# A hybrid block on one core: buffers shared across phases, residual rows added to beta by their transfer, last group stored by tiles

## The chip, the cores and the metric

The kernel runs on one core of one Trainium2 chip. The metric is the device time of one execution in microseconds (us). Five engines run their own instruction streams: TensorE (PE, with its weight loads as PEld), VectorE (DVE), ScalarE (ACT), GpSimd (POOL) and SyncE (SP). They meet only through semaphores. Transfers are issued by SP, ACT or POOL and carried out by 16 DMA engines that all queues share.

## The reference, cut to what matters

```python
x = attn_a(x)      # Mamba-2 style mixer: 16 heads of 64, state 64
x = ffn(x)         # below
x = attn_b(x)      # mixer: 64 heads of 16, state 128
x = ffn(x)         # the same weights again

# ffn, per batch b of 4, 1024 rows of 512, fp32
x1     = layer_norm(x)                                   # rows of x
t      = layer_norm(last row of x1, in_gamma, in_beta)
th     = t @ agg_w + agg_b
for step in range(4):                                    # K_STEPS
    n  = layer_norm(th, pn_gamma, pn_beta)
    th = th + gelu(n @ d1_w + d1_b) @ d2_w + d2_b        # d1_w 512x2048, d2_w 2048x512
msg    = th @ bc_w + bc_b                                # one vector per batch
gate   = sigmoid(x1 @ gate_w + gate_b)
out    = x + layer_norm(x1 + gate * msg) * out_gamma + out_beta
```

This is the shape of the computation as the kernel does it. All data are float32: 4096 rows of 512, so one pass over x is 8 MB.

## The kernel before, in words

The four phases A, F, B, F follow one another, each a block of its own that all engines enter and leave together. x goes through DRAM between phases (`x_mid`). Within a mixer phase the work goes by 16 supertiles of 256 rows, with a loop in the middle and the first, the last but one and the last supertile written out.

An F phase has three parts.

*Opening.* SP issues the loads in a fixed order: the four last rows (`last`), agg_w, x_in[0], d1_w (4 MB), gate_w, d2_w (4 MB), x_in[1], bc_w, the gamma and beta rows, and the residual rows `x_res` of group 0. DVE normalises the last rows twice (`normalise_last`, each time with a power on POOL between), then takes the statistics of the first group's 512 rows (`statistics(0)`), then waits for PE's transposes of the last rows.

*Recurrence.* Four steps on four vectors, each a chain PE, DVE, POOL, DVE, PE (L1590, the product with d1_w), DVE, PE, ACT, PE (L1605, the product with d2_w), DVE, PE. Beside this chain PE works ahead on the groups: transposes of normalised rows (`prepare`, L1510) and single matmuls of the gate (`logits`, L1521), dealt out by the table PRODUCTS. PE takes its instructions in their written order, so what stands beside the chain can also hold it up.

*Groups.* Eight groups of 512 rows. For group n PE transposes the gated rows back (`back`, L1544), DVE takes statistics of them, multiplies the gate (`gated`), subtracts the mean (`centre`, L1770) and adds the residual (`finish`, L1779). POOL computes the scale (`out_scale`, L1889 and L1890). The residual rows sit in two buffers that take turns, x_res (even groups) and bc_w's buffer (odd groups). Each is loaded by SP after the store of the group two before (`load_res`, L1474), then POOL adds the beta row to it in four operations (`add_beta`, L1882), then `finish` uses it and SP stores it (`store`, L1478).

Phase B's SP starts with the loads of its first rows and of w_in (4.7 MB, L119 to L124), and w_out.

## Time and profile before

| | us |
|---|---|
| three runs | 3009.7, 3011.1, 3011.82 (median 3011.1) |
| the profiled execution's own time | 3011.85 |
| its span | 3010.1 |
| PE busy | 2792.6 (93%) |
| DVE busy | 2018.7 (67%) |
| ACT busy | 1248.8 (41%) |
| POOL busy | 953.3 (32%) |
| phase A begins and ends | 0, 1143 |
| first F phase | 1143 to 1393 |
| phase B | 1393 to 2760 |
| second F phase | 2760 to 3010 |

The phase borders are read from the first instruction of each phase in the timeline (1143.13, 1393.43 and 2760.79 us). A matmul in float32 of 128x512 shows as two records. "Idle before" in brackets at the end of a row is how long the engine had waited, and for whom. A DMA's row on SPq or ACTq is its issue, not its transfer.

### The profile page before, as it was taken

The numbers are of one execution on the slowest core, as the hardware profiler recorded it, in microseconds if no ns is written. First come the engines' busy times: TensorE is split into PE (matmuls) and PEld (weight loads), VectorE is DVE, ScalarE is ACT, GpSimd is POOL, SyncE is SP. The second block draws the span as 40 slices with busy tenths as digits, with TensorE's granted clock in tenths as the row PEclk, the third lists the DMA queues.
The fourth block names the chain that finished last, engine by engine and source line by source line (L and its number), as shares of the span: only waits on it lengthen the run. The fifth ranks groups of instructions, "written<-read, shape, count | busy, mean of one in ns | idle before, by whom it ended". The sixth has DMA issues, their size and how long they took to land. (4 is left out here: it accounts for less than half of the span.)

```text
span 3010.1 us, 54346 instructions
## 1 busy us (share of the span) xinstructions
PE 2792.6 (93%) x19824; PEld 1848.6 (61%) x19824; DVE 2018.7 (67%) x3697; ACT 1248.8 (41%) x2098; POOL 953.3 (32%) x618
## 2 busy tenths in 40 slices
PE   6999999999999996995899999999999999996896
PEld 5677666666667753454666666666666666663443
DVE  4656666656666662377777777777777777774267
ACT  3344443344434431341454444544445544442241
POOL 2322223222332230242333333333333333332134
PEclk9999999999999997997999999999999999997898
DMA  4000000000000006144000000000000000003433
GB/s 126 15 29 21 21 21 21 28 28 21 21 23 26 14 19 234 42 149 185 11 23 21 21 21 17 17 21 21 17 14 17 21 21 21 14 13 126 143 108 131
DMA packets 80674, 140.16 MB, mean 47 GB/s; under 512 B 18121, under 2 KB 18633, under 8 KB 79569
## 3 DMA queue, kind: packets, MB, share of 16 engines
q1 hardware_dynamic: 70448, 126.44, 12.2%
q10 hardware_dynamic: 10144, 12.64, 1.3%
q8 instruction: 51, 0.84, 0.1%
q14 instruction: 31, 0.25, 0.0%
HBM read 104.98 MB, written 33.55 MB: 46 GB/s over the span
## 5 line engine op out<-in xcount | busy, mean ns | idle before, releaser
L565 PE MATMUL work<-b_xnT,b_w_in 128*128 128x256 f32 x2304 | 548.3, 388 | 4.0 <-DVE b_parts L1077 3.9
L565 PE MATMUL work<-a_xnT,a_w_in 128*128 128x256 f32 x2176 | 501.6, 386 | 6.0 <-DVE a_parts L1077 4.7
L565 PEld LDWEIGHTS work<-b_xnT,b_w_in 128*128 128x128 f32 x2304 | 425.2, 191 | 87.3 <-issue 20.0
L565 PEld LDWEIGHTS work<-a_xnT,a_w_in 128*128 128x128 f32 x2176 | 409.4, 192 | 78.1 <-issue 18.3
L1117 DVE TENSOR_TENSOR b_decay<-b_decay,b_gt 128x1024 f32<-128x1024 f32 x256 | 354.3, 1421 | 28.4 <-ACT b_decay L841 24.4
L841 ACT ACTIVATE b_decay<-seg 128x1024 f32<-128x1024 f32 x256 | 251.3, 1021 | 174.8 <-PE seg L691 174.0
L1327 POOL TENSOR_TENSOR a_y<-a_y,a_skip 128x1024 f32<-128x1024 f32 x32 | 103.4, 3230 | 513.9 <-DVE a_y L1106 513.9
L1292 POOL TENSOR_TENSOR b_rhs<-b_l_side,of_head 128x1024 fp32r<-128x1024 f32 x32 | 82.0, 2563 | 578.8 <-DVE b_l_side L1086 578.8
L996 DVE SCALAR_TENSOR_TENSOR b_cv<-b_pre,b_conv_w,b_cv 128x256 f32<-128x256 f32 x480 | 222.5, 492 | 46.0 <-ACT b_cv L787 38.1
L672 PE MATMUL work<-b_w_out,b_yz 128*128 128x512 f32 x512 | 228.5, 599 | 8.3 <-DVE b_y L1106 8.3
L996 DVE SCALAR_TENSOR_TENSOR a_cv<-a_pre,a_conv_w,a_cv 128x256 f32<-128x256 f32 x432 | 189.7, 482 | 65.6 <-ACT a_cv L787 59.9
L672 PE MATMUL work<-a_w_out,a_yz 128*128 128x512 f32 x512 | 229.4, 601 | 3.5 <-DVE a_y L1106 3.4
L672 PEld LDWEIGHTS work<-b_w_out,b_yz 128*128 128x128 f32 x512 | 95.3, 191 | 118.0 <-issue 108.3
L672 PEld LDWEIGHTS work<-a_w_out,a_yz 128*128 128x128 f32 x512 | 95.7, 192 | 113.7 <-issue 108.8
L1117 DVE TENSOR_TENSOR a_decay<-a_decay,a_gt 128x1024 f32<-128x1024 f32 x64 | 151.1, 2383 | 11.5 <-ACT a_decay L841 11.0
L793 ACT COPY a_z_raw<-work 128x256 f32<-128x256 f32 (+1 forms) x96 | 42.2, 440 | 272.1 <-PE work L565 272.1
L1327 POOL TENSOR_TENSOR b_y<-b_y,b_skip 128x1024 f32<-128x1024 f32 x32 | 95.8, 2992 | 185.4 <-DVE b_y L1106 185.4
L705 PE MATMUL y<-b_decay,b_xdt 128*32 128x128 f32 x4096 | 139.8, 276 | 0.0
L705 PEld LDWEIGHTS y<-b_decay,b_xdt 128*32 128x32 f32 x4096 | 104.0, 110 | 52.3 <-issue 39.4
L1521 PE MATMUL y<-f_x1T,f_gate_w 128*128 128x512 f32 x256 | 130.1, 640 | 1.5 <-ACT f_x1T L1646 1.5
L786 ACT COPY b_pre<-work 128x256 f32<-128x256 f32 x160 | 59.8, 374 | 154.5 <-PE work L565 154.5
L1521 PE MATMUL y<-f_d_w,f_gate_w 128*128 128x512 f32 x256 | 111.5, 592 | 0.0
(311 smaller groups left out, 4617.2 us busy)
## 6 DMA issues: line engine op xcount, KB each, us to landing
f_d_w<-in_L_ffn_d_w SPq DMA_DIRECT2D x4, 4096.0 KB, 24.4
f_x_in<-x_mid ACTq DMA_DIRECT2D x12, 1024.0 KB, 6.1
a_x_in<-in_L_attn_a_x SPq DMA_DIRECT2D x16, 512.0 KB, 3.7
a_x_res<-in_L_attn_a_x SPq DMA_DIRECT2D x32, 256.0 KB, 2.6
x_mid<-a_x_res SPq DMA_DIRECT2D x32, 256.0 KB, 2.0
f_x_res<-x_mid SPq DMA_DIRECT2D x8, 1024.0 KB, 5.6
f_bc_w<-x_mid SPq DMA_DIRECT2D x8, 1024.0 KB, 5.5
b_x_in<-x_mid SPq DMA_DIRECT2D x16, 512.0 KB, 3.6
```

The source lines that it names most:

```text
L565: mm = nc.tensor.matmul(dst, w_in[:, k, col:col + m], xnT[:, k, :], start=(k == 0), stop=(k == KD - 1))
L672: mm = nc.tensor.matmul(bank[:, :], yz[:, k, :], w_out[:, k, :], start=(k == 0), stop=(k == KE - 1))
L705: mm = nc.tensor.matmul(ybank[32 * q:32 * q + 32, slot * P:(slot + 1) * P], xdt[:, j, 4 * slot + q, 16 * odd:16 * odd + 32], decay[:, slot ...
L786: nc.scalar.copy(pre[0:m, b, HALO:], bank[0:m, 0:SUP])
L793: nc.scalar.copy(z_raw[:, got[0]:got[-1] + 1, :], sec.bank(name)[:, 0:len(got) * SUP].rearrange("p (b t) -> p b t", t=SUP)).then_inc(z_rea ...
L841: nc.scalar.activation(decay[:, slot_buffer(j, s)].rearrange("p h l -> p (h l)"), seg[s % 2][:, :], ACT.Exp).then_inc(exp_done, 1)
L996: ins = nc.vector.scalar_tensor_tensor(out=cv[0:m, b, :], in0=pre[0:m, b, t:t + SUP], scalar=conv_w[0:m, b, t:t + 1], in1=cv[0:m, b, :], o ...
L1117: nc.vector.tensor_tensor(d, d, gt[:, j].unsqueeze(1).to_broadcast([P, 8, P]), ALU.mult).then_inc(m_ready, 1)
L1292: nc.gpsimd.tensor_tensor(rhs[1][:], l_side[:, 1].unsqueeze(1).to_broadcast([P, 8, P]), c["of_head"][:].unsqueeze(2).to_broadcast([P, 8, P ...
L1327: nc.gpsimd.tensor_tensor(y1[:], y1[:], skip[:], ALU.add).then_inc(y1x_ready, 1)
L1521: mm = nc.tensor.matmul(ybank[:, (m % 2) * 512:(m % 2 + 1) * 512], gate_w[:, k, m * P:(m + 1) * P], x1T[n][:, k, :], start=(k == 0), stop= ...
```

## The change: what it does

1. **Shared buffers.** Five buffers ("arenas" w, cv, pre, z, x) now live over all phases. Mixer phases keep w_in, cv, pre, z_raw, x_in and xn in them; F phases keep d1_w, agg_w, gate_w, both x_in buffers and two small row buffers. So a phase can be loaded while the one before still runs: a mixer's SP loads agg_w, gate_w, d1_w and x_in[0] during its last supertile, and the first F phase's SP loads phase B's first rows and w_in after the load for group 7.
2. **The opening of F.** SP's queue starts with the last rows, d2_w, x_in[1], bc_w. DVE does `statistics(0)` and `aggregate(0)` before it normalises the last rows. POOL does `in_scale(0)` first. PE transposes group 0 ahead of the last rows' transposes; before, this stood in step 0.
3. **Residual rows.** SP fills x_res with the beta row, repeated over all rows (1 MB). Then POOL issues a transfer that adds the rows of x to it (`accum_op=ALU.add`). The four POOL additions per group are gone; `finish` waits for the transfer.
4. **Last group.** It is stored by four transfers of 256 KB, each as soon as its tile is done.

```diff
+def ffn_inputs(arena):
+    return {"d1": cut(arena["w"], 0, KD, 2048), "agg": cut(arena["cv"], 0, KD, DM), "gate": cut(arena["pre"], 0, KD, DM),
+            "x_in": [cut(arena["z"], 0, 4, DM), cut(arena["x"], 0, 4, DM)],
+            "rows": [arena["w"][:, KD * 2048 + k * 512:KD * 2048 + (k + 1) * 512] for k in range(2)]}
...
# mixer_phase, SP
-                if not early:
-                    load_in(sp, x_in, w_in, xs_src, w, x_loaded, xbc_loaded)
-                    load_z(sp, w_in, w, z_loaded)
+                def load_next_phase():
+                    to, fw = ffn_inputs(arena), c["ffn_w"]
+                    sp.wait_ge(silu_done, FREE + 2 * NSUP)
+                    sp.wait_ge(halo_done, FREE + NSUP)
+                    sp.dma_start(to["agg"], ...).then_inc(before("w_agg"), 16)
+                    sp.dma_start(to["gate"], ...).then_inc(before("w_gate"), 16)
+                    sp.wait_ge(work_full, last().full("zzb"))
+                    sp.dma_start(to["d1"], ...).then_inc(before("w_d1"), 16)
+                    sp.wait_ge(zs_done, NSUP)
+                    for t in stored:
+                        sp.wait_ge(t, STORED + 16 * 2)
+                    sp.dma_start(to["x_in"][0], by_group(x_dst)[0]).then_inc(before("x_loaded0"), 16)
...
                 step(NSUP - 2, None, NSUP - 3, NSUP - 1)
+                load_next_phase()
                 step(NSUP - 1, None, NSUP - 2, None)
...
# ffn_phase, SP
-                def load_res(n):
+                def load_beta(n):
...
-                    sp.dma_start(x_res[n % 2][:], src_t[n]).then_inc(res_loaded[n % 2], 16)
+                    sp.dma_start(x_res[n % 2][:], w["out_beta"].rearrange("(a t d) -> a t d", a=1, t=1).to_broadcast(
+                        [P, NT, DM])).then_inc(beta_loaded[n % 2], 16)
...
+                        for t in range(NT):
+                            sp.wait_ge(done, NT * n + t + 1)
+                            sp.dma_start(dst_t[n][:, t], x_res[n % 2][:, t]).then_inc(stored[n % 2], 16)
...
+                    sp.wait_ge(x1_ready, NT * GROUPS)
+                    sp.wait_ge(o_full, NT * 5)
+                    sp.wait_ge(stored[0], 16)
+                    load_in(sp, to_x, to_w, by_supertile(x_dst), mw, signals("x_loaded"), signals("xbc_loaded"))
+                    load_z(sp, to_w, mw, signals("z_loaded"))
...
                     if n + 2 < GROUPS:
-                        load_res(n + 2)
+                        load_beta(n + 2)
+                    if n == 5 and following:
+                        load_next_phase()
...
# ffn_phase, POOL
-                def add_beta(n):
-                    pool.wait_ge(res_loaded[n % 2], 16 * (n // 2 + 1))
-                    for t in range(NT):
-                        nc.gpsimd.tensor_tensor(x_res[n % 2][:, t, :], x_res[n % 2][:, t, :], beta_row[:], ALU.add
-                                                ).then_inc(res_beta, 1)
+                def add_rows(n):
+                    pool.wait_ge(beta_loaded[n % 2], 16 * (n // 2 + 1))
+                    pool.dma_start(x_res[n % 2][:], src_t[n], accum_op=ALU.add).then_inc(res_loaded[n % 2], 16)
```

How the order of instructions moves, at three places. On DVE at the opening of the first F phase, before (f_l_stats and f_last belong to the four last rows, f_stats and f_mv to the rows of group 0):

```order
L1723 BN_STATS f_l_stats<-f_last 4x6 [waits f_last_loaded,f_v_chain]
L1727 TENSOR_SCALAR f_last<-f_last,f_l_mv,f_l_r 4x512 [waits f_rows_r]
L1736 BN_STATS f_stats<-f_x_in 128x6 [waits f_x_loaded0]
L1736 BN_STATS f_stats<-f_x_in 128x6 x3
L1794 TENSOR_TENSOR f_tt<-seg,in_gamma 128x4x4 [waits ffn_loaded,f_lastT_full,f_v_chain]
L1795 TENSOR_TENSOR f_tt<-f_tt,in_beta 128x4x4 [waits f_v_chain]
L1743 MEMSET f_carrier 128x1
L1745 BN_AGGR f_mv<-f_stats 128x2 x4
```

The same place now (shared_z is x_in[0]):

```order
L1802 BN_STATS f_stats<-shared_z 128x6 [waits f_x_loaded0,f_v_chain]
L1802 BN_STATS f_stats<-shared_z 128x6 x3
L1809 MEMSET f_carrier 128x1 [waits f_v_chain]
L1811 BN_AGGR f_mv<-f_stats 128x2 x4
L1789 BN_STATS f_l_stats<-f_last 4x6 [waits f_last_loaded]
L1793 TENSOR_SCALAR f_last<-f_last,f_l_mv,f_l_r 4x512 [waits f_rows_r]
L1861 TENSOR_TENSOR f_tt<-seg,in_gamma 128x4x4 [waits ffn_loaded,f_lastT_full]
```

The statistics of group 0 and their aggregation moved ahead of the two normalisations. On PE at the same opening, before (L1563 transposes the last rows, L1550 is the product with agg_w, L1510 the transposes of group 0):

```order
L1563 MATMUL seg<-ident,f_last 128x4 [waits f_rows_ready]
L1550 MATMUL seg<-f_agg_w,f_tt 32x512 [waits f_w_agg,f_t_ready]
L1557 MATMUL seg<-f_batch_of,f_delta_rows 128x4 [waits f_delta_ready]
L1573 MATMUL seg<-f_th,mean_w 128x4 [waits f_th_ready]
L1510 MATMUL work<-ident,f_x 128x128 [waits f_x1_ready]
L1510 MATMUL work<-ident,f_x 128x128 [waits f_x1T_ready,f_x1_ready]
L1521 MATMUL y<-f_x1T,f_gate_w 128x512 [waits f_x1T_ready,f_w_gate]
L1582 MATMUL seg<-f_sq,mean_w 128x4 [waits f_sq_ready]
```

And now:

```order
L1576 MATMUL work<-ident,f_x 128x128 [waits f_x1_ready]
L1576 MATMUL work<-ident,f_x 128x128 [waits f_x1T_ready,f_x1_ready]
L1631 MATMUL seg<-ident,f_last 128x4 [waits f_rows_ready]
L1616 MATMUL seg<-shared_cv,f_tt 32x512 [waits f_w_agg,f_t_ready]
L1623 MATMUL seg<-f_batch_of,shared_w 128x4 [waits f_delta_ready]
L1641 MATMUL seg<-f_th,mean_w 128x4 [waits f_th_ready]
L1587 MATMUL y<-f_x1T,shared_pre 128x512 [waits f_x1T_ready,f_w_gate]
L1648 MATMUL seg<-f_sq,mean_w 128x4 [waits f_sq_ready]
```

The transposes of group 0 left the stretch between the mean and the variance of step 0 and stand first. On SP at the end of the first F phase, before:

```order
L1478 DMA x_mid<-f_bc_w 128x4x512 [waits f_done]
L1474 DMA f_bc_w<-x_mid 128x4x512 [waits f_stored1]
L1478 DMA x_mid<-f_x_res 128x4x512 [waits f_done]
L1478 DMA x_mid<-f_bc_w 128x4x512 [waits f_done]
L1463 UNCONDITIONAL_BRANCH [waits f_stored1,f_stored0]
```

And now:

```order
L1533 DMA x_mid<-f_bc_w 128x4x512 [waits f_done]
L1527 DMA f_bc_w<-in_L_ffn_out_beta 128x4x512 [waits f_stored1]
L146 DMA shared_x<-x_mid 128x2x512 [waits f_stored0,f_o_full,f_x1_ready]
L147 DMA shared_w<-in_L_attn_b_in_proj_w 128x4x1344
L151 DMA shared_w<-in_L_attn_b_in_proj_w 128x4x1024
L1533 DMA x_mid<-f_x_res 128x4x512 [waits f_done]
L1537 DMA x_mid<-f_bc_w 128x512 [waits f_done] x4
L1516 UNCONDITIONAL_BRANCH [waits f_stored1,f_stored0]
```

Three loads of phase B, 5.2 MB, now stand on SP's queue ahead of the stores of groups 6 and 7.

## Rows read from the trace of the kernel before

**Rows 1.** The page, part 1: busy time, share of the span, instructions.

```profile
PE 2792.6 (93%) x19824; PEld 1848.6 (61%) x19824; DVE 2018.7 (67%) x3697; ACT 1248.8 (41%) x2098; POOL 953.3 (32%) x618
```

**Rows 2.** Windows: stretch, length, busy PE PEld DVE ACT POOL, PEclk, DMA, GB/s.

```profile
1160.00:1170.00 10.00, 9.23 (x34) 7.09 (x35) 0.60 (x4) 2.34 (x4) 0.30 (x1) 0.50 1.04 388
...
2877.00:2980.00 103.00, 101.77 (x370) 55.52 (x371) 82.52 (x163) 42.10 (x67) 48.02 (x50) 1.00 0.38 132
```

**Rows 3.** Timeline, opening of the first F phase: start, us, engine, line, operation, [idle before].

```profile
1148.42 20.46 SPq L1467 DMA_DIRECT2D f_x_in<-x_mid  x1
...
1149.45 1.86 PE L1563 MATMUL seg<-ident,f_last 4*128 4x4 f32 x8 [9.73 <-DVE f_last L1727]
...
1151.68 2.47 DVE L1736 BATCH_NORM_STATS2 f_stats<-f_x_in 128x6 f32<-128x512 f32 x4 [2.29 <-DMA f_x_in<-x_mid]
...
1154.63 1.93 PE L1550 MATMUL seg<-f_agg_w,f_tt 128*32 128x512 f32 x8 [3.32 <-DVE f_tt L1795]
...
1161.23 3.80 PE L1510 MATMUL work<-ident,f_x 128*128 128x128 f32 x16
...
1167.64 1.71 PE L1582 MATMUL seg<-f_sq,mean_w 128*128 128x4 f32 x8
...
1173.60 3.64 PE L1590 MATMUL seg<-f_d_w,f_tt 128*32 128x512 f32 x32
...
1182.03 2.48 DVE L1736 BATCH_NORM_STATS2 f_stats<-f_x_in 128x6 f32<-128x512 f32 x4 [10.90 <-DMA f_x_in<-x_mid]
...
1187.90 4.45 PE L1605 MATMUL seg<-f_d_w,f_hid 128*32 128x512 f32 x32
```

**Rows 4.** Timeline, step 2 (first row) and step 3 of the same recurrence.

```profile
1218.10 0.18 DVE L1812 TENSOR_TENSOR f_cen<-f_cen,f_m_r 128x16 f32<-128x16 f32 x1 [1.12 <-POOL f_m_r L1899]
...
1239.92 4.96 POOL L1882 TENSOR_TENSOR f_x_res<-f_x_res,f_out_beta_row 128x512 f32<-128x512 f32 x4
1239.98 1.23 DVE L1812 TENSOR_TENSOR f_cen<-f_cen,f_m_r 128x16 f32<-128x16 f32 x1 [1.12 <-POOL f_m_r L1899]
1241.25 1.19 DVE L1813 TENSOR_TENSOR f_tt<-f_cen,pn_beta 128x16 f32<-128x16 f32 x1
1242.49 3.64 PE L1590 MATMUL seg<-f_d_w,f_tt 128*32 128x512 f32 x32 [1.22 <-DVE f_tt L1813]
...
1249.28 3.64 PE L1605 MATMUL seg<-f_d_w,f_hid 128*32 128x512 f32 x32
```

**Rows 5.** Timeline, last supertile of phase A: the residual rows of its last tile.

```profile
1109.76 0.33 SPq L523 DMA_DIRECT2D a_x_res<-in_L_attn_a_x  x1
```

**Rows 6.** Timeline, second F phase, last groups.

```profile
2980.42 5.08 DVE L1779 SCALAR_TENSOR_TENSOR f_bc_w<-f_tq,f_r_out,f_bc_w 128x512 f32<-128x512 f32 x4
...
3002.65 2.74 DVE L1779 SCALAR_TENSOR_TENSOR f_bc_w<-f_tq,f_r_out,f_bc_w 128x512 f32<-128x512 f32 x4 [0.48 <-POOL f_r_out L1890]
```

**Rows 7.** The chain that ended last, in order of time: start, us, what.

```profile
2985.53 4.27 DMA out<-f_bc_w
...
2989.81 5.54 DMA f_bc_w<-x_mid
```

**Rows 8.** DMA issues: count, KB each, median us from issue to landing.

```profile
x_mid<-a_x_res SPq DMA_DIRECT2D x32, 256.0 KB, 2.0
```

**Rows 9.** Source L1640, window 1150 to 1165: one load of 1 MB on ACT's queue.

```profile
DMA to landing us min/median/max: 9.8/9.8/9.8
```

**Rows 10.** Timeline, end of the first F phase and start of phase B.

```profile
1328.92 4.58 DVE L1779 SCALAR_TENSOR_TENSOR f_bc_w<-f_tq,f_r_out,f_bc_w 128x512 f32<-128x512 f32 x4
...
1362.65 5.97 DVE L1779 SCALAR_TENSOR_TENSOR f_bc_w<-f_tq,f_r_out,f_bc_w 128x512 f32<-128x512 f32 x4
...
1393.43 0.38 SPq L119 DMA_DIRECT2D b_x_in<-x_mid  x1
...
1397.08 0.69 DVE L956 BATCH_NORM_STATS2 b_stats<-b_x_in 128x6 f32<-128x512 f32 x1 [8.57 <-DMA b_x_in<-x_mid]
...
1404.05 3.67 PE L594 MATMUL work<-b_w_in,b_xnT 128*128 128x64 f32 x16 [1.81 <-DMA b_w_in<-in_L_attn_b_in_proj_w]
```

More of the change, by code:

```diff
@@ L158, in build_constants @@
     c["ffn_w"] = ffn_w
+    c["res_loaded"] = {f"f{n}": [ctx.enter_context(nc.semaphore(f"f{n}_res_loaded{k}")) for k in range(2)] for n in (1, 3)}
     c["weights"] = weights
@@ L227, in build_constants, with mixer_phase @@
     return c
-def mixer_phase(nc, sig, before, cfg, c, early, later, psum, x_src, x_dst, w):
+def mixer_phase(nc, sig, before, cfg, c, arena, later, psum, x_src, x_dst, w):
     H, HP, N, NS = cfg.H, cfg.HP, cfg.N, cfg.slots
@@ L253, in sb @@
             return ctx.enter_context(nc.sbuf_tensor(f"{cfg.tag}_{name}", shape, dt))
-        w_in = early["w_in"] if early else sb("w_in", [P, KD, cfg.proj])
+        x_in, w_in = mixer_inputs(arena, cfg)
         w_out = sb("w_out", [P, KE, DM])
@@ L261, in mixer_phase @@
         lhs, rhs = sb("lhs", [P, 2, P], F32R), [sb(f"rhs{k}", [P, 8, P], F32R) for k in range(2)]
-        x_in = early["x_in"] if early else sb("x_in", [P, 2, DM])
         x_res = sb("x_res", [P, 2, DM])
@@ L537, in step @@
                         load_res(nxt, 0)
+                def load_next_phase():
+                    to, fw = ffn_inputs(arena), c["ffn_w"]
+                    sp.wait_ge(silu_done, FREE + 2 * NSUP)
+                    sp.wait_ge(halo_done, FREE + NSUP)
+                    sp.dma_start(to["agg"], fw["agg_w"].rearrange("(k p) n -> p k n", p=P)).then_inc(before("w_agg"), 16)
+                    sp.dma_start(to["gate"], fw["gate_w"].rearrange("(k p) n -> p k n", p=P)).then_inc(before("w_gate"), 16)
+                    sp.wait_ge(work_full, last().full("zzb"))
+                    sp.dma_start(to["d1"], fw["d1_w"].rearrange("(k p) n -> p k n", p=P)).then_inc(before("w_d1"), 16)
+                    sp.wait_ge(zs_done, NSUP)
+                    for t in stored:
+                        sp.wait_ge(t, STORED + 16 * 2)
+                    sp.dma_start(to["x_in"][0], by_group(x_dst)[0]).then_inc(before("x_loaded0"), 16)
                 load_x(1)
@@ L1397, in sb @@
             return ctx.enter_context(nc.sbuf_tensor(f"{tag}_{name}", shape, dt))
-        d1_w, d2_w = sb("d1_w", [P, KD, HID]), sb("d2_w", [P, KH, DM])
-        agg_w, bc_w, gate_w = (sb(k, [P, KD, DM]) for k in ("agg_w", "bc_w", "gate_w"))
+        loaded = ffn_inputs(arena)
+        d1_w, agg_w, gate_w, x_in = loaded["d1"], loaded["agg"], loaded["gate"], loaded["x_in"]
+        d2_w, bc_w = sb("d2_w", [P, KH, DM]), sb("bc_w", [P, KD, DM])
         in_gamma, in_beta, pn_gamma, pn_beta = (c["ffn"][k] for k in ("in_gamma", "in_beta", "pn_gamma", "pn_beta"))
         agg_b, d2_b, d1_b, gate_b, bc_b = (c["ffn"][k] for k in ("agg_b", "d2_b", "d1_b", "gate_b", "bc_b"))
-        gamma_row, beta_row = sb("out_gamma_row", [P, DM]), sb("out_beta_row", [P, DM])
-        x_in, x_res0 = [sb(f"x_in{k}", [P, NT, DM]) for k in range(2)], sb("x_res", [P, NT, DM])
+        gamma_row = sb("out_gamma_row", [P, DM])
+        x_res0 = sb("x_res", [P, NT, DM])
         x1 = sb("x1", [P, NT, DM])
@@ L1559, in to_columns @@
                     mm.then_inc(col_full, 1)
+                for t in range(NT):
+                    prepare(0, t)
                 pe.wait_ge(rows_ready, 1)
@@ L1786, in _ @@
                                              mybir.AxisListType.X, ALU.add))
+                link(statistics(0))
+                aggregate(0)
                 dve.wait_ge(last_loaded, 16)
@@ L1789, in _ @@
                 normalise_last(1, EPS)
-                link(statistics(0))
                 dve.wait_ge(lastT_full, 1)
```

102 lines of the change are left out of this document (56 added, 46 removed).

## The prediction, made before the result was known

> **What bounds the kernel now.** I read the page first: PE is busy for 93% of the span [rows 1], so only places where PE stands idle, or works at half clock, can give time back. The change leaves the work of the mixer phases alone; it touches the borders between phases, the opening and recurrence of each F phase, and the last groups. The windows come next. In the middle of the second F phase's groups PE is busy for 101.77 of 103 us at full clock [rows 2]. There the loop is PE's, and nothing that POOL or DVE saves there counts. At the opening of F it is otherwise: the granted clock is 0.50, that is 1.2 GHz, while the 16 DMA engines move 388 GB/s, their whole share [rows 2]. The timeline says what this costs [rows 3]. SP needs 20.46 us to issue x_in[1], because its queue is full of d1_w, gate_w and d2_w. DVE's `statistics(1)` stands ahead of the copy that the recurrence needs, and waits 10.90 us for that x_in[1]. PE's product with d1_w ends about 1177.2, and its product with d2_w starts only at 1187.90. In step 3, where nothing is waited for, the same distance from the start of one product to the start of the other is 1249.28 - 1242.49 = 6.8 us [rows 4]; here it is 1187.90 - 1173.60 = 14.3. Last come the chain and the timeline of the final groups [rows 6, 7], which are a ring of store, load, addition and finish.
>
> **The opening, part by part.** Removed from the opening's queue: agg_w, x_in[0], d1_w, gate_w, 7 MB of the roughly 12 MB that had to pass before x_in[1]. With d2_w and x_in[1] alone, 5.2 MB at 388 GB/s take 13.5 us and a little latency, so both are there by 1143.5 + 16 = 1159.5, before DVE asks. DVE now takes the statistics (2.47 us, [rows 3]) and their aggregation (about 0.5) ahead of the normalisations, so the last rows are ready at 1149.4 + 3.0 = 1152.4. PE does the transposes of group 0 first. They take 3.80 us at 1.2 GHz [rows 3] and two of four wait for an ACT copy; I put their end at 1153.6. The last rows' transposes take 1.86 [rows 3], so L1550 starts near 1156.0, 1.4 us later than before. From it to the end of the mean took 1161.23 - 1154.63 = 6.6 us, which gives 1162.6. The variance then followed 1167.64 - 1161.23 = 6.4 us later; the transposes and the wait for their copy (3.80 + 0.6) are gone from this stretch and one gate matmul at half clock (2.05) stays, so it starts at 1164.7, 2.9 us earlier. PE rose from the low clock near 1172 before. If it rises at the same moment now, the three gate matmuls up to L1590 lose about 1 us of that, and L1590 starts at 1171.7 instead of 1173.60. Then the undisturbed 6.8 us of step 3 [rows 4] lead to L1605 at 1178.5 instead of 1187.90, which is 9.4 us. L1605 itself took 4.45 because the clock had fallen during the wait; at full clock it takes 3.64 [rows 3, 4], 0.8 more. Together 10.2 us in the first F phase. The second F phase has the same rows shifted, so 10.2 again.
>
> **Step 3.** Before, POOL's first addition of beta (4.96 us) ran beside two tiny DVE operations of the chain, which took 1.23 and 1.19 us [rows 4], where the same kind takes 0.18 [first row of rows 4]. POOL will only issue a transfer there. Saved: 1.05 + 1.01 = 2.1 us per F phase. Were POOL's work of writing the transfer's descriptors to disturb DVE as much, this would be nothing; two tiny operations cannot lose more than they do now, so the bounds are 0 and 2.1. I take 2.1.
>
> **The preloads themselves.** In phase A (and B) the loads of 7.3 MB go on SP's queue in the last supertile, ahead of the store of the last but one supertile and of the last tile's residual rows. Those rows were issued at 1109.76 [rows 5] and are used in the very last tile, just before the phase ends at 1143. A full queue of 7.3 MB is 19 us at 388 GB/s, and most of it is issued before 1097, so it has drained by about 1112. I cost this at nothing; the cover is some 30 us.
>
> **The ring of the last groups.** For a buffer the path was: finish(n-2), store 4.27, load 5.54, four POOL additions, finish(n) [rows 6, 7]. Now: finish, store 4.3, beta transfer (1 MB; 5.5 as the load of the same size), adding transfer, finish. No row shows an adding transfer. Its bounds: not less than the plain load, 5.5; above, it reads and writes the destination as well, so twice that, 11, and 1 us for POOL's issue. I take 8, and keep 5.5 and 12, and a worse case as a rival. In the steady groups the ring has two group times, 1362.65 - 1328.92 = 33.7 us from finish(3) to finish(5) [rows 10], and needs 2.7 + 4.3 + 5.5 + 8 = 20.5, so it is hidden behind PE.
>
> At the end the groups come closer together. Second F phase: finish(5) ran from 2980.42 for 5.08 us beside POOL's additions; the last finish, undisturbed, takes 2.74 [rows 6]. It now ends at 2983.2, and everything on DVE after it is 2.3 us earlier; the wait of 0.48 for POOL [rows 6] goes too, since the scale of group 7 no longer stands behind additions. So DVE could start finish(7) at 3002.65 - 2.3 - 0.5 = 2999.8. The ring says 2983.2 + 4.3 + 5.5 + 8 = 3001.0, which is later and therefore decides. The new last wait is DVE's, for the adding transfer. finish(7) ends at 3003.7, and a store of 256 KB takes 2.0 [rows 8] and 0.4 to issue: 3006.1. Before: 3002.65 + 2.74 + 4.3 = 3009.7. Saved 3.6 us; with 5.5 for the transfer 4.8 (DVE decides), with 12 a loss of 0.4.
>
> **End of the first F phase and start of B.** finish(5) there took 5.97 [rows 10], so it ends 3.2 us earlier, at 1365.4; beta(7) has landed at 1375.2. But SP now also puts 5.4 MB of loads for phase B behind beta(7) and ahead of the stores of groups 6 and 7. What a transfer of 1 MB on another queue takes beside such a backlog stands in [rows 9]: 9.8 us. So finish(7) starts at 1385.2 and ends at 1388, as late as before. The stores wait behind the loads: beta 1.05, loads 5.4, two stores 2.1, adding transfer 1.05, in all 9.6 MB from 1370 on, at 388 GB/s 24.7 us, so the phase ends near 1396 instead of 1393.4 [rows 10], a loss of 3. In B, DVE no longer waits for its rows (1397.08 - 1393.43 = 3.65 us) and PE not for w_in (1.81 us, of which 1.2 remained as the copies of the transposes) [rows 10]; gain 4.6. Net 1.6, and I say 1, with -4 and +5 as bounds.
>
> A rule of the Trainium skill speaks against this change: "DMA: Bandwidth & Descriptors", section "Issuing engines are not separate DMA queues", says that transfers started by scalar, sync or gpsimd run on the same 16 DMA engines and interleave. The trace agrees with its 9.8 us beside a full queue. The same page gives in "Anatomy of one DMA" a fit for plain transfers from GpSimd, 2.0 us plus bytes over 436 GB/s, which is 4.4 us for 1 MB; with it DVE would decide the end of the last phase and the sum would be 1.2 us lower. No row here shows such a transfer.
>
> **Sum.** 2 x 10.2 + 2 x 2.1 + 3.6 + 1 = 29.2 us. The profiled execution took 3011.85 us, so 2982.6; it lies 0.75 above the median of the three runs, so I say 2982.
>
> **Rivals.**
> *The adding transfer is slow.* In favour: nothing in this trace shows one, it carries 512 pieces of 2 KB, and it touches the destination twice. Against: its size is modest. At the end of a phase the ring misses DVE by (length - 6.9) us, since finish(7) could follow finish(5) by 19.4 us and the ring needs 12.5 plus the transfer. It decides over the whole saving (24.6 from opening and step 3, 4.6 from B's start, about 1.5 by small stores) when both phases lose more than 15 us, at about 22 us, four times the plain load; from there the steady groups begin to be late too. At 27 us finish(7) comes 3 x 39.5 - 87.5 = 31 us late in each F phase (three turns of the ring from finish(1)), and the kernel takes 3011.85 - 30.7 + 62 = 3043: slower.
> *A middling adding transfer of 12 to 18 us.* The two ends lose 4 to 10 us more each than I forecast: 2990 to 3002. For it speaks that the first F phase already has a backlog beside it.
> *The clock.* PE's opening runs at 1.2 GHz, and the low clock could last through step 0, or the chain drop to it again (the recurrence has idle stretches). The two products, transposes and gate matmuls of step 0 cost about 4 to 5 us more per F phase: 2991. Against: PE now has no idle stretch of 8 us in step 0.
> *Something else was late anyway.* If d2_w (now alone, but 4 MB) or the loads behind it still hold `statistics(1)`, the opening gives only 3 us: 2 x 7 more, 2996. The bandwidth sum above speaks against.
>
> **How the numbers follow.** Forecast 0.60 (its own range 2975 to 2989), clock 0.14, middling transfer 0.14, loads late anyway 0.05, slow transfer 0.07, of which 0.05 ends slower. What a measurement can tell from no change is about 0.2%, 6 us. Only the slow transfer or a heap of two rivals ends above 3005, so faster 0.92, same 0.03, slower 0.05. The range for 8 in 10 takes in the forecast, the clock and the middling case's lower part: 2973 to 2996.
>
> **What would show it.** The second `statistics` of the opening should have no wait for x_in, L1605 of step 0 should start 35 to 36 us after the phase's first instruction (before 44.8), PE's windows there should hold no idle stretch, and the two tiny operations of step 3 should take 0.2 us each. The adding transfers should land in 6 to 12 us, and DVE's one wait at the end should be for the last of them. Phase B's first statistics should start at once. I am wrong if a buffer's finishes come more than 35 us apart, if the phase border F to B moves by more than 5 us, or if the two F phases differ in their openings.

## The result, and the profile after

The changed kernel takes 2997.3 us (median of five runs, 2992.4 to 3002.2); the kernel before took 3009.7 us beside it (five runs, 3007.1 to 3011.8). The ratio is 0.996, with a 95% interval of 0.9945 to 0.9974: 12.4 us faster, where 29.2 were forecast (2982). The time lies 1.3 us above the top of the range, 2996.

The profiled execution took 2996.89 us with a span of 2995.2, 15.0 less than the profiled 3011.85. Phase by phase (an F phase begins with POOL's memset of f_root; phase B with SP's first issue in it, of x_in in the kernel before and of w_out now; finish(5) is DVE's last step on group 5, the line of [rows 6]):

| us | before | after | gained | forecast |
|---|---|---|---|---|
| phase A | 1143.1 | 1142.3 | 0.8 | 0 |
| first F phase, start to finish(5) | 219.5 | 208.1 | 11.4 | 12.3 |
| first F phase, finish(5) to the end | 30.8 | 42.0 | -11.2 | -3.6 |
| phase B | 1367.4 | 1362.3 | 5.1 | 4.6 |
| second F phase, start to finish(5) | 219.6 | 207.5 | 12.1 | 12.3 |
| second F phase, finish(5) to the end | 29.7 | 33.0 | -3.3 | 3.6 |

The forecast of -3.6 is the prediction's net of 1 for the end of the first F phase and B's start, less its 4.6 for B. Everything ahead of the last groups came as forecast, and both ends of the F phases came out worse. The windows of the same stretches as [rows 2]:

```profile
1160.00:1170.00 10.00, 9.73 (x28) 6.74 (x29) 2.56 (x10) 0.00 (x0) 1.01 (x1) 0.50 0.70 266
2857.00:2960.00 103.00, 100.95 (x376) 55.58 (x373) 75.84 (x161) 43.92 (x68) 25.65 (x33) 1.00 0.74 178
```

At the opening the DMA engines carry less (0.70 of their time, before 1.04), and at 1168 DVE already does its second statistics. In the steady groups PE is the bound as before, POOL's work has halved (48.02 to 25.65), and the DMA engines are busy for 0.74 of the time instead of 0.38 while they move 178 GB/s instead of 132: a third more bytes take twice the engine time. The landing times below say what the two new kinds of transfer cost. The opening, beside [rows 3]:

```profile
1165.08 1.71 PE L1648 MATMUL seg<-f_sq,mean_w 128*128 128x4 f32 x8
...
1171.86 3.64 PE L1656 MATMUL seg<-shared_w,f_tt 128*32 128x512 f32 x32
...
1178.64 3.64 PE L1671 MATMUL seg<-f_d_w,f_hid 128*32 128x512 f32 x32
...
1168.48 2.46 DVE L1802 BATCH_NORM_STATS2 f_stats<-shared_x 128x6 f32<-128x512 f32 x4
```

The wait of 10.90 us is gone from `statistics(1)`, and the product with d2_w (now L1671) starts 36.3 us into the phase, before 44.8. In step 3, beside [rows 4], the tiny operations take 0.17 us although POOL is busy issuing a transfer at that moment:

```profile
1228.96 1.51 POOL L1947 DMA_DIRECT2D f_x_res<-x_mid  x1
1229.04 0.17 DVE L1878 TENSOR_TENSOR f_cen<-f_cen,f_m_r 128x16 f32<-128x16 f32 x1 [1.12 <-POOL f_m_r L1963]
1229.25 0.17 DVE L1879 TENSOR_TENSOR f_tt<-f_cen,pn_beta 128x16 f32<-128x16 f32 x1
```

The end of the second F phase (timeline; beside [rows 6]):

```profile
2962.22 2.73 DVE L1845 SCALAR_TENSOR_TENSOR f_bc_w<-f_tq,f_r_out,f_bc_w 128x512 f32<-128x512 f32 x4
2964.47 1.35 POOL L1947 DMA_DIRECT2D f_x_res<-x_mid  x1 [5.22 <-DMA f_x_res<-in_L_ffn_out_beta]
2964.98 0.38 SPq L1533 DMA_DIRECT2D out<-f_bc_w  x1
2970.32 0.37 SPq L1527 DMA_DIRECT2D f_bc_w<-in_L_ffn_out_beta  x1
2975.73 2.74 DVE L1845 SCALAR_TENSOR_TENSOR f_x_res<-f_tq,f_r_out,f_x_res 128x512 f32<-128x512 f32 x4 [2.52 <-issue]
...
2979.78 1.36 POOL L1947 DMA_DIRECT2D f_bc_w<-x_mid  x1 [9.63 <-DMA f_bc_w<-in_L_ffn_out_beta]
2989.86 2.74 DVE L1845 SCALAR_TENSOR_TENSOR f_bc_w<-f_tq,f_r_out,f_bc_w 128x512 f32<-128x512 f32 x4 [5.63 <-issue]
2990.64 2.32 SPq L1537 DMA_DIRECT2D out<-f_bc_w  x4
```

Read it as the ring. Group 5's store goes from 2964.98 to 2970.32 (5.3 us), the beta transfer from there to 2979.78 (9.5), the adding transfer from there to 2989.86 (10.1). DVE's last two finishes wait 2.52 and 5.63 us. The profile writes "issue" there and names no releaser; it does the same in experiment 4, where POOL's transfer is a plain one. That finish(7) waits for the adding transfer follows from that transfer's landing, 10.0 us after its issue at 2979.78 (the source view of L1947 in a window around it), 0.1 us ahead of the finish.

The steady groups came near the same wait. Group 5's turn of the ring in this phase starts with finish(3) at 2928.49:

```profile
2929.67 1.35 POOL L1947 DMA_DIRECT2D f_x_res<-x_mid  x1 [4.15 <-DMA f_x_res<-in_L_ffn_out_beta]
2931.25 0.38 SPq L1533 DMA_DIRECT2D out<-f_bc_w  x1
...
2941.47 0.37 SPq L1527 DMA_DIRECT2D f_bc_w<-in_L_ffn_out_beta  x1
...
2949.59 1.35 POOL L1947 DMA_DIRECT2D f_bc_w<-x_mid  x1 [6.84 <-DMA f_bc_w<-in_L_ffn_out_beta]
```

The store took 10.2 us, the beta transfer 8.1, and the adding transfer 11.3 from its issue to its landing. It landed 32.4 us after finish(3) had started, 1.3 us ahead of finish(5). The end of the first F phase and the start of phase B, beside [rows 10]:

```profile
1350.41 2.73 DVE L1845 SCALAR_TENSOR_TENSOR f_bc_w<-f_tq,f_r_out,f_bc_w 128x512 f32<-128x512 f32 x4
...
1358.23 0.37 SPq L1527 DMA_DIRECT2D f_bc_w<-in_L_ffn_out_beta  x1
1358.72 1.71 SPq L146 DMA_DIRECT2D shared_x<-x_mid  x1
1360.47 1.26 SPq L147 DMA_DIRECT2D shared_w<-in_L_attn_b_in_proj_w  x1
1361.77 0.66 SPq L151 DMA_DIRECT2D shared_w<-in_L_attn_b_in_proj_w  x1
...
1368.72 1.34 POOL L1947 DMA_DIRECT2D f_bc_w<-x_mid  x1 [10.38 <-DMA f_bc_w<-in_L_ffn_out_beta]
1384.72 2.74 DVE L1845 SCALAR_TENSOR_TENSOR f_bc_w<-f_tq,f_r_out,f_bc_w 128x512 f32<-128x512 f32 x4 [12.62 <-issue]
...
1392.37 0.39 SPq L549 DMA_DIRECT2D b_w_out<-in_L_attn_b_out_proj_w  x1
1393.48 0.69 DVE L1006 BATCH_NORM_STATS2 b_stats<-shared_x 128x6 f32<-128x512 f32 x1 [6.02 <-issue]
...
1399.40 3.01 PE L644 MATMUL work<-shared_w,b_xnT 128*128 128x64 f32 x13 [0.77 <-ACT b_xnT L821]
```

Here beta takes 10.5 us, and the adding transfer beside phase B's loads 16.0 (1368.72 to 1384.72). Phase B's first product starts 7.0 us after the phase does, before 10.6. The page's landing times (count, KB each, median us), where before had 5.6 and 5.5 for the load of the same tiles:

```profile
f_x_res<-in_L_ffn_out_beta SPq DMA_DIRECT2D x8, 1024.0 KB, 10.6
f_x_res<-x_mid POOLq DMA_DIRECT2D x8, 1024.0 KB, 10.3
f_bc_w<-in_L_ffn_out_beta SPq DMA_DIRECT2D x8, 1024.0 KB, 8.2
```

### The profile page after: what moved, and what is told of

The parts are those of the page before. It is cut to its first block and busy times, and to the rows that moved or that the text cites. A ratio compares the mean times of both kernels' runs of the same rounds, so it can differ in the third digit from the quotient of the medians.

```text
span 2995.2 us, 54304 instructions
## 1 busy us (share of the span) xinstructions
PE 2783.4 (93%) x19824; PEld 1846.5 (62%) x19824; DVE 1996.2 (67%) x3697; ACT 1249.8 (42%) x2098; POOL 886.3 (30%) x570
## 5 line engine op out<-in xcount | busy, mean ns | idle before, releaser
L615 PE MATMUL work<-b_xnT,shared_w 128*128 128x256 f32 x2304 | 548.5, 389 | 6.2 <-DVE b_parts L1127 6.1
L615 PE MATMUL work<-a_xnT,shared_w 128*128 128x256 f32 x2176 | 501.0, 386 | 5.7 <-DVE a_parts L1127 4.4
L615 PEld LDWEIGHTS work<-b_xnT,shared_w 128*128 128x128 f32 x2304 | 425.4, 191 | 89.4 <-issue 20.0
L615 PEld LDWEIGHTS work<-a_xnT,shared_w 128*128 128x128 f32 x2176 | 409.0, 191 | 77.6 <-issue 18.3
L843 ACT COPY shared_z<-work 128x256 f32<-128x256 f32 (+1 forms) x192 | 85.0, 442 | 414.2 <-PE work L615 414.2
L1046 DVE SCALAR_TENSOR_TENSOR shared_cv<-shared_pre,b_conv_w,shared_cv 128x256 f32<-128x256 f32 x480 | 222.4, 492 | 46.3 <-ACT shared_cv L837 38.5
L836 ACT COPY shared_pre<-work 128x256 f32<-128x256 f32 x304 | 113.7, 374 | 286.7 <-PE work L615 286.7
L1046 DVE SCALAR_TENSOR_TENSOR shared_cv<-shared_pre,a_conv_w,shared_cv 128x256 f32<-128x256 f32 x432 | 189.7, 482 | 65.1 <-ACT shared_cv L837 59.5
L1587 PE MATMUL y<-f_x1T,shared_pre 128*128 128x512 f32 x256 | 128.9, 636 | 0.0
L1384 POOL TENSOR_TENSOR b_xw<-b_xdt,b_e 128x512 f32<-128x512 f32 x64 | 106.1, 1677 | 0.0
## 6 DMA issues: line engine op xcount, KB each, us to landing
f_x_res<-in_L_ffn_out_beta SPq DMA_DIRECT2D x8, 1024.0 KB, 10.6
f_x_res<-x_mid POOLq DMA_DIRECT2D x8, 1024.0 KB, 10.3
```

Source lines behind the costliest of these rows:

```text
L615: mm = nc.tensor.matmul(dst, w_in[:, k, col:col + m], xnT[:, k, :], start=(k == 0), stop=(k == KD - 1))
L836: nc.scalar.copy(pre[0:m, b, HALO:], bank[0:m, 0:SUP])
L843: nc.scalar.copy(z_raw[:, got[0]:got[-1] + 1, :], sec.bank(name)[:, 0:len(got) * SUP].rearrange("p (b t) -> p b t", t=SUP)).then_inc(z_rea ...
L1046: ins = nc.vector.scalar_tensor_tensor(out=cv[0:m, b, :], in0=pre[0:m, b, t:t + SUP], scalar=conv_w[0:m, b, t:t + 1], in1=cv[0:m, b, :], o ...
L1384: ins = nc.gpsimd.tensor_tensor(xw4[:, :, odd, :], xdt[:, j, :, 32 * odd:32 * odd + HP], e4[:, :, odd:odd + 1].to_broadcast([P, H // 2, HP ...
L1587: mm = nc.tensor.matmul(ybank[:, (m % 2) * 512:(m % 2 + 1) * 512], gate_w[:, k, m * P:(m + 1) * P], x1T[n][:, k, :], start=(k == 0), stop= ...
```

## The experiments

Stage times of the profiled executions, in us: F1 and F2 are the F phases, "to 5" runs from the phase's start to finish(5), "tail" from there to its end.

| kernel | F1 to 5 | F1 tail | B | F2 to 5 | F2 tail |
|---|---|---|---|---|---|
| before | 219.5 | 30.8 | 1367.4 | 219.6 | 29.7 |
| after | 208.1 | 42.0 | 1362.3 | 207.5 | 33.0 |
| 1 old residual path | 209.6 | 34.0 | 1364.7 | 209.6 | 27.4 |
| 2 late loads for B | 208.3 | 34.3 | 1363.5 | 207.4 | 32.8 |
| 3 rows for beta | 208.2 | 42.2 | 1362.2 | 207.5 | 33.7 |
| 4 plain on POOL | 208.3 | 40.2 | 1363.1 | 208.1 | 28.9 |
| 5 old opening | 204.4 | 42.7 | 1362.3 | 207.3 | 34.2 |
| 6 rows from x_in | 208.1 | 24.8 | 1362.3 | 207.7 | 24.6 |
| 7 old residual, late loads | 207.9 | 27.8 | 1363.2 | 209.0 | 27.4 |
| 8 before with tile stores | 219.8 | 27.8 | 1365.1 | 218.6 | 27.6 |
| 9 as 6, again | 210.5 | 24.8 | 1362.4 | 208.1 | 24.6 |
| 10 rows from x_in, late loads | 208.2 | 24.9 | 1364.3 | 208.2 | 24.7 |
| 11 as 7, again | 209.5 | 27.9 | 1363.8 | 209.3 | 27.5 |
| 12 rows from x_in, old opening | 206.7 | 24.8 | 1362.4 | 204.3 | 24.6 |

Phase A, whose work no experiment touches, was 1137.3 to 1144.0 us long in these profiles, and a kernel's own runs spread over up to 10 us; so the stages decide below, and medians only where a run has an interval. Phase B too differs by up to 2.4 us between kernels that treat it alike (the changed kernel and 1, before and 8), so small differences there are read from the start of its first product with w_in.

**1. The old residual path in the changed kernel.**

```diff
-  sp.dma_start(x_res[n % 2][:], w["out_beta"]....to_broadcast([P, NT, DM]))
+  sp.dma_start(x_res[n % 2][:], src_t[n])
-  pool.dma_start(x_res[n % 2][:], src_t[n], accum_op=ALU.add)
+  for t in range(NT):
+      nc.gpsimd.tensor_tensor(x_res[n % 2][:, t, :], x_res[n % 2][:, t, :], beta_row[:], ALU.add)
   ...                            # beta_row loaded again, finish waits for the additions
```

> The changed kernel with the residual rows as before: a plain load of the rows, then four additions of the beta row on POOL. Theory (the gain was lost in the ring of the last groups, where the two transfers take 9.5 and 10.1 us in place of 5.5 and 5.8): from the start of finish(5) to the end, the second F phase falls from 33.0 us back to about 28 (before: 29.7, less some 2 us by the small stores); in the first F phase from 42.0 to about 34 (before 30.8; the backlog of phase B's loads stays ahead of the stores). Recurrence 2.1 us longer in each F phase. In all 8 to 10 us under the changed kernel, near 2988. Rival (the small stores or SP's order are to blame, not the transfers): the second F phase keeps its 33 us, and the kernel is 4 us slower than the changed one, near 3001.

Measured: 2984.8 us (before beside it 3009.05; ratio 0.9917, 0.9903 to 0.993), some 12 us under the changed kernel. Tails 34.0 and 27.4. The last finish:

```profile
2980.23 2.74 DVE L1845 SCALAR_TENSOR_TENSOR f_bc_w<-f_tq,f_r_out,f_bc_w 128x512 f32<-128x512 f32 x4 [0.49 <-POOL f_r_out L1956]
```

The two transfers lost 8.0 and 5.6 us at the ends, and gave back 1.5 and 2.0 by finish(5). So this part of the change costs 10.1 us in the F phases. Behind phase A the profiled executions differ by 7.7, since phase B ran 2.4 us longer here with its first product at the same 7.0 us; that part stays open. The theory held, and the median came out 2 to 4 us better than it said.

**2. Phase B's loads behind the last stores.**

```diff
-  if n == 5 and following:
-      load_next_phase()
   ...
+  if following:                  # behind the stores of all groups
+      load_next_phase()
```

> The changed kernel with phase B's loads in the first F phase moved behind the last stores. Theory (the backlog stretches the last adding transfer of the first F phase from 10 to 16 us and holds back the stores): adding transfer for group 7 lands in 10 us, finish(5) to the end of the phase 35 to 36 us instead of 42; B's product with w_in then waits for its load some 4 us; in all 2 to 4 us under the changed kernel, near 2994. Rival (the backlog only takes from idle engines): the first F phase stays at 41 to 42, and B loses 4 to 6 us, near 3002. The second F phase is the same in both.

Measured: 2988.8 us, ratio 0.994 (0.9927 to 0.9954). The first tail shrank from 42.0 to 34.3, the adding transfer of group 7 from 16.0 to 11.5; B's first product starts 8.2 us into its phase instead of 7.0:

```profile
1365.60 1.34 POOL L1947 DMA_DIRECT2D f_bc_w<-x_mid  x1 [9.29 <-DMA f_bc_w<-in_L_ffn_out_beta]
1377.12 2.74 DVE L1845 SCALAR_TENSOR_TENSOR f_bc_w<-f_tq,f_r_out,f_bc_w 128x512 f32<-128x512 f32 x4 [4.82 <-issue]
```

The backlog costs nearly 8 us in the tail, against 1.2 that it gives to B. The theory's mechanism held, and it had the size too small: 6.7 us behind phase A where it said 2 to 4.

**3. Rows instead of beta in the first transfer.** This kernel adds the rows of x twice and leaves out_beta out.

```diff
-  sp.dma_start(x_res[n % 2][:], w["out_beta"]....to_broadcast([P, NT, DM]))
+  sp.dma_start(x_res[n % 2][:], src_t[n])
```

> The changed kernel, but the 1 MB transfer that fills x_res with the repeated beta row reads the group's own 512 rows of x instead (so the rows are added twice and beta not at all). Theory A (reading one row of 2 KB 512 times is what is slow): these transfers land in 5.5 to 6 us where no other transfer runs, against 7.8 at best with beta, and the one for group 7 of the second F phase in 6 to 8 instead of 9.5. Theory B (it is slow because it meets the adding transfer of the other buffer): 7.8 at best and 9.5 for group 7, as with beta.

Measured, one run: 2992.8 us. Landing of the first transfer, min/median/max, in the changed kernel and then in this one:

```profile
DMA to landing us min/median/max: 7.8/8.9/15.6
```
```profile
DMA to landing us min/median/max: 5.2/5.5/13.5
```

The same megabyte, into the same buffers by the same queue, takes 3.4 us longer if all its pieces come from one row of 2 KB. The one for group 7 of the second F phase took 5.7 us, a little under the 6 to 8 of theory A. The tail did not shrink with it (33.7). Group 6's adding transfer is now issued 1.1 us ahead of group 5's store (0.5 in the changed kernel), and this store took 10.6 us (5.3), from its issue to that of the next load into its buffer:

```profile
2959.08 1.35 POOL L1946 DMA_DIRECT2D f_x_res<-x_mid  x1 [4.64 <-DMA f_x_res<-x_mid]
2960.18 0.38 SPq L1532 DMA_DIRECT2D out<-f_bc_w  x1
...
2970.81 0.37 SPq L1527 DMA_DIRECT2D f_bc_w<-x_mid  x1
```

**4. A plain transfer in place of the adding one, on POOL's queue.** This kernel leaves out_beta out.

```diff
-  pool.dma_start(x_res[n % 2][:], src_t[n], accum_op=ALU.add)
+  pool.dma_start(x_res[n % 2][:], src_t[n])
```

> The changed kernel, but POOL's transfer of the residual rows is a plain one that overwrites the destination (beta is left out). Theory A (the adding itself costs): these transfers land in 5.5 to 7 us, against 8.9 at best and 10.3 median with adding, and the second F phase's wait of finish(7), 5.6 us, falls to about 2. Theory B (POOL's issue costs, adding nothing): 9 to 10 us as before, and POOL's issue 1.35 us each in both.

Measured, one run: 2989.9 us, second tail 28.9 (33.0). The wait of finish(7) fell from 5.63 to 4.11 us, not to 2: the beta transfer ahead still took 8.6 us and group 5's store 5.7. The first tail stayed at 40.2, since the plain transfer for group 7, beside phase B's loads, took 10.5. Landing times, and the instructions, with the adding and then without (duration in ns, min/median/max):

```profile
L1947 POOL DMA_DIRECT2D f_bc_w<-x_mid x8: 1285/1345/1364, 1253.7 to 2979.8; - x8
...
DMA to landing us min/median/max: 8.9/10.3/15.9
```
```profile
L1947 POOL DMA_DIRECT2D f_bc_w<-x_mid x8: 748/820/828, 1251.5 to 2976.4; - x8
...
DMA to landing us min/median/max: 5.9/6.1/10.5
```

The adding itself costs 4.2 us for this megabyte, and 0.5 us of POOL's time for each issue.

**5. The old order of the opening, with the preloads.**

```diff
-  link(statistics(0))
-  aggregate(0)
   dve.wait_ge(last_loaded, 16)
   normalise_last(0, LN_EPS)
   normalise_last(1, EPS)
+  link(statistics(0))
   ...                            # aggregate(0), transposes and scale of group 0 later, as before
```

> The changed kernel with the opening's order of before on DVE, PE and POOL (the last rows normalised before group 0's statistics, group 0's transposes inside step 0, the aggregation and the scale of group 0 later); the preloads stay. Theory A (the preloads took the wait away and the order is worth little): the first product with d2_w starts 37 to 39 us after the phase's first instruction (36.3 with the new order, 44.8 before), 1 to 3 us lost per F phase, 3000 to 3003. Rival B (the order is what keeps PE from idling and raises its clock early): 42 us or more, 6 us per F phase, 3009.

Measured: 2996.3 us (before beside it 3007.3; ratio 0.996, 0.9944 to 0.9975), the ratio of the changed kernel. Both theories fell: both expected the old order to lose time. The product with d2_w started 31.5 us into the first F phase and 35.5 into the second (36.3 and 35.7 in the changed kernel). By windows of 1 to 2 us, PE's clock rose from 0.50 to 1.00 at 19.2 us into the first F phase and 27.8 into the second (29.3 and 28.0 in the changed kernel). First the window 1160 to 1165 in the changed kernel, still at the low level, then the same in this one:

```profile
1160.00:1165.00 5.00, 4.73 (x16) 3.69 (x17) 0.61 (x4) 0.00 (x0) 0.00 (x0) 0.50 1.06 405
```
```profile
1160.00:1165.00 5.00, 4.23 (x21) 3.06 (x20) 0.00 (x0) 2.35 (x4) 0.00 (x0) 0.74 1.05 405
```

**6. Groups 6 and 7 take their residual rows from x_in.** Both groups' rows are still in the two x_in buffers when the ring would fetch them again.

```diff
+  def residual(n):
+      return {GROUPS - 2: x_in[0], GROUPS - 1: x1[:]}.get(n, x_res[n % 2][:])
   # POOL, iteration 4
+  add_beta(x_in[0], x_in[0])     # four additions of beta_row, for group 6
   out_scale(n)
+  add_beta(x1, x_in[1])          # and for group 7
   # SP: load_beta and add_rows only up to group 5; load_next_phase at n == 4
```

> The changed kernel, but groups 6 and 7 need no transfer for their residual rows: the rows of group 6 are still in x_in[0] and those of group 7 in x_in[1]; POOL adds out_beta to them in eight additions in its iteration 4 (group 6 in place, group 7 into x1, which is free by then), and both groups are stored from there. Groups 0 to 5 keep beta transfer and adding transfer; phase B's loads are issued one group earlier, with no transfer that DVE waits for behind them. Theory A (the ring of transfers is all that lengthened the ends): no wait before the last two finishes. The second F phase's tail, from finish(5) to the end, goes from 33.0 to 33.0 - 2.5 - 5.6 = 24.8 us, the first one's from 42.0 to 25 to 28; in all 8 + 15 = 23 us under the changed kernel, 2971 to 2977. Rival B (the ends are set by PE or by POOL's scale once the ring is gone, or the eight additions slow DVE in the steady groups so that it is late): a wait for PE or POOL before finish(7) and only 10 us gained, near 2987.

Measured: 2978.3 us (before beside it 3007.3; ratio 0.99, 0.9885 to 0.9916). The tails are 24.8 and 24.6, with no wait ahead of the last two finishes, here in the second F phase:

```profile
2945.78 2.73 DVE L1854 SCALAR_TENSOR_TENSOR f_bc_w<-f_tq,f_r_out,f_bc_w 128x512 f32<-128x512 f32 x4
...
2956.68 2.73 DVE L1854 SCALAR_TENSOR_TENSOR shared_z<-f_tq,f_r_out,shared_z 128x512 f32<-128x512 f32 x4
...
2965.09 2.73 DVE L1854 SCALAR_TENSOR_TENSOR f_x<-f_tq,f_r_out,f_x 128x512 f32<-128x512 f32 x4
```

The median lay 1 us above the bracket, the profiled execution (2972.1) inside it.

**7. Old residual path and late loads together** (the edits of 1 and 2).

> The changed kernel with the kernel before's residual path (one load, four additions on POOL) and with phase B's loads issued behind the last stores; arenas, preloads of the F phases, new opening and small last stores stay. Theory A (the adding transfer and the backlog are two separate costs of the first F phase's end, both already seen one at a time): the first F phase's tail goes to 29 us or less (34.0 with the old residual path alone, 34.3 with late loads alone, 30.8 before, less 2 for the small stores), phase B loses 1.2 us against early loads, the second F phase is that of the old residual path, 27.4 us: 5 - 1.2 = about 4 us under the kernel with the old residual path alone, so near 2981. Rival B (with the old path the backlog costs nothing, since POOL has no transfer that it could meet; the 34.0 are the additions'): tail 33 to 34, and the time 2985 to 2987.

Measured: 2976.6 us, ratio 0.9898 (0.9882 to 0.9914). The first tail fell from 34.0 to 27.8, so with the old path too the backlog costs 6 us, and by another way than I had thought: finish(7) starts 22.7 us after finish(5) with early loads and 22.3 with late ones, but from it to the end of the phase the stores take 11.3 and 5.6 us. First the kernel of experiment 1, then this one:

```profile
1372.55 2.74 DVE L1845 SCALAR_TENSOR_TENSOR f_bc_w<-f_tq,f_r_out,f_bc_w 128x512 f32<-128x512 f32 x4 [0.49 <-POOL f_r_out L1956]
...
1383.84 0.39 SPq L549 DMA_DIRECT2D b_w_out<-in_L_attn_b_out_proj_w  x1
```
```profile
1368.38 2.74 DVE L1845 SCALAR_TENSOR_TENSOR f_bc_w<-f_tq,f_r_out,f_bc_w 128x512 f32<-128x512 f32 x4 [0.49 <-POOL f_r_out L1956]
...
1373.94 0.37 SPq L549 DMA_DIRECT2D b_w_out<-in_L_attn_b_out_proj_w  x1
```

Theory A holds, its mechanism only in part. The time is 4 us better here than it said, and 2981.7 when the same kernel ran again (11), as it said.

**8. The kernel before with tile stores in the last group.**

```diff
+  for t in range(NT):
+      sp.wait_ge(done, NT * n + t + 1)
+      sp.dma_start(dst_t[n][:, t], x_res[n % 2][:, t])
```

> The kernel before with one edit: the last group of each F phase is stored by tiles of 256 KB, each as soon as DVE has finished it. Theory A: the last store's landing goes from 4.3 to about 2.3 us, so each F phase ends 2 us earlier, tails 28.8 and 27.7 instead of 30.8 and 29.7; 3007 in all. Rival B: four issues on SP and four completions eat it, and the tails stay within 0.5 us.

Measured, one run: 3001.2 us, where 3007 was expected, with a phase B 2.3 us shorter that the edit doesn't touch; tails 27.8 and 27.6, 3.0 and 2.1 less. The small stores are worth what was taken (2 us); in the first tail, 0.8 of the 3.0 is a finish(5) that ran 5.14 instead of 5.97.

**9 to 11. Versions 6 and 7 side by side, and 6 with late loads.** 9 is the kernel of 6 again, 11 that of 7. The edit of 10 is that of 2 on top of 6.

> The kernel whose groups 6 and 7 take their residual rows from x_in, again, beside the one with the old residual path and late loads. The two measured the same (2978.3 and 2976.6 us), while their profiled executions differ by 7.8 us in the three stages behind phase A (2827.5 and 2835.3 us). Theory A (the stages are what they are, and the medians of five and four runs hid it through the clock's luck and the length of phase A): a median 3 to 8 us under the other kernel's, 2970 to 2976. Rival B (the profiled execution was a lucky one, and the eight additions in POOL's iteration 4 cost what the ring gave): the same median within 2 us.

> The kernel with the old residual path and late loads, again, for comparison on the same chip: 2975 to 2981 by theory A and by rival B; tails 27.8 and 27.4 us as before.

> Groups 6 and 7 take their residual rows from x_in, and phase B's loads are issued behind the last stores. Theory A (the backlog of phase B's loads costs only through the transfers that DVE waits for, and here there are none): the first F phase's tail stays at 24.8 us, within 0.3, and phase B alone gets longer, by 1.2 us; 1 us slower than with early loads. Rival B (the loads also hold up the last stores, so that late loads shorten the tail by 1 us or more): the same time or faster.

Measured beside one another: 9 took 2973.1 us (ratio 0.988, 0.9863 to 0.9896), 11 took 2981.7 (0.9908, 0.9892 to 0.9925) and 10 took 2973.8 (0.9877, 0.986 to 0.9893). Version 6 is 8.7 us under version 7, which is what the stages had said (7.8), and I put the tie of 6 and 7 down to chance. With the ring gone from the last two groups and the early loads issued a group sooner, late loads leave the tail as it is (24.9 and 24.8), and B's first product starts 8.3 us into its phase instead of 7.0. But the early loads now stand beside the adding transfer of group 5. It took 14.6 us in 9 and 15.0 in 12, and finish(5) waited for it in the first F phase:

```profile
1348.39 2.74 DVE L1854 SCALAR_TENSOR_TENSOR f_bc_w<-f_tq,f_r_out,f_bc_w 128x512 f32<-128x512 f32 x4 [2.16 <-issue]
```

In 6 it took 11.7 us and nobody waited; with late loads (10) there was no such wait. So in 9 the backlog costs 2.2 us ahead of finish(5), where the tail doesn't show it, and gives B 1.2 at the mark; 9 and 10 end even. A backlog costs where a transfer that somebody waits for meets it.

**12. Version 6 with the old opening.**

> The kernel whose groups 6 and 7 take their residual rows from x_in, with the old order of the opening. With the new order the first product with d2_w started 35.6 to 36.5 us into both F phases in every profile so far; in the one profile with the old order it started at 31.5 in the first F phase, where the granted clock rose 8 us earlier, and at 35.5 in the second. Theory A (that clock was chance, the order is worth nothing): 35.3 to 36.3 in both F phases, and a time within 2 us of the same kernel with the new order (2973.1 and 2978.3 us in two sessions). Rival B (the old order raises the clock earlier in the first F phase): 31 to 32 again there, and 4 us faster.

Measured: 2968.5 us (2963.3 to 2968.6), before beside it 3011.9; ratio 0.9855 (0.9838 to 0.9871). The product with d2_w started at 31.3 and 31.4 us. So theory A, chance, fell: of four openings in the old order with preloads three had it at 31.3 to 31.5, of 20 in the new order none was under 35.6. Its finish(5) of the first F phase waited 2.46 us beside the early loads, as in 9. Its windows of the first opening, where the clock rises to 1.00 at 18.9 us into the phase:

```profile
1155.00:1160.00 5.00, 3.95 (x18) 3.87 (x19) 1.04 (x3) 2.93 (x4) 0.24 (x2) 0.50 1.05 398
1160.00:1165.00 5.00, 4.23 (x20) 3.12 (x18) 0.26 (x2) 2.35 (x4) 0.00 (x0) 0.72 1.05 405
1165.00:1170.00 5.00, 5.00 (x31) 2.30 (x33) 2.88 (x7) 0.69 (x1) 1.01 (x1) 1.00 1.04 277
```

This version has the lowest time of all: 1.5% under the kernel before, and 1.0% under the changed kernel by their ratios.

## Why the prediction was wrong

**The opening and step 3: right.** 24.6 us forecast for both F phases, 23.5 measured, with the marks close to where they were expected (no wait; the product with d2_w at 36.3 and 35.7 us for 35 to 36; 0.17 us). One inner term had the wrong sign. I gave part of the gain to the new order on DVE and PE; experiments 5 and 12 show that the gain is there without it, and that in three of four openings the old order was 4 to 5 us ahead of the new one at that mark, with an earlier rise of the clock.

**Preloads in phase A at nothing: right.** No wait appeared there, and A's length is in the spread of all profiles. **Phase B's start: right,** 5.1 for 4.6, though part of that is luck: at the first product with w_in 3.6 us are gained (10.6 to 7.0), and the other 1.5 lie later in a phase that varies by up to 2.4.

**The ring of the last groups: this step failed, in the size of its terms.** The mechanism stood in the text (finish, store, beta, adding transfer, finish; DVE's wait at the end is for the last of them), and so did the rival that is nearest to what happened, the middling adding transfer. But the sum took 4.3 + 5.5 + 8 = 17.8 us for the three transfers, and the second F phase shows 5.3 + 9.5 + 10.1 = 24.9. That is the 7 us between a gain of 3.6 and a loss of 3.3. The worst term was the one held for safe: I priced beta as "5.5 as the load of the same size", though its source is one row of 2 KB read 512 times, and no row showed such a read at all; experiment 3 gives 8.9 against 5.5. For the adding transfer 8 was my middle between 5.5 and 12, and experiment 4 shows 10.3 against 6.1 plain on the same queue. The fit for plain GpSimd transfers that the prediction took from the Trainium skill ("DMA: Bandwidth & Descriptors", "Anatomy of one DMA"), 4.4 us, is below even the shortest plain one here, 5.9 in experiment 4.

**The steady groups: right that nothing waits, by luck.** The prediction gave the ring there 20.5 of 33.7 us. In the changed kernel's second F phase the turn up to group 5 needed 32.4, with a store of 10.2 us behind the issue of the other buffer's adding transfer; the margin was 1.3 us, and in experiments 9 and 12, with phase B's loads beside that turn, it was gone.

**End of the first F phase: the same step, and a backlog priced with the wrong transfer.** I took 9.8 us for the adding transfer beside the loads, from a plain load of the same size beside a backlog; an adding transfer took 16.0. With beta's 10.5 instead of 5.5 it was 34.3 us from the start of finish(5) to that of finish(7), instead of the 22.6 that the prediction's times give; the stores behind it were 3 us quicker than I had feared. That is 8.6 us, of which the rounding to a net of 1 had covered 1.0, so 7.6 more than forecast; experiment 2 puts nearly 8 us of that tail down to the loads.

**The chances.** The forecast had 0.60 and the middling adding transfer, "2990 to 3002", only 0.14, and the range was cut in that case's middle. The time fell into that case's window, but its condition, 12 to 18 us, held only at the end of the first F phase (16.0); in the second, beta's price made up the rest. Of the three signs of being wrong that the prediction named none appeared: the border from F to B moved by only 1.1 us, because a gain of 11.4 and a loss of 11.2 met there. A border inside the F phase would have shown it. Two prices that no row showed, each in a ring that ends both F phases, were worth a range up to 3002.
